# First feed-forward weight loaded and summed one element later; constants of the later stages loaded in the sixth element's round

## The reference, cut to what matters

```python
x = x + _L0_xattn_ref(_layernorm(x, axis=-1), ctx_2048, mask_BxS2_bk0)
x = x + _L0_ffn_ref(_layernorm(x, axis=-1), L0_ffn_w1, L0_ffn_w2, L0_ffn_w3)
x = x + _L1_xattn_ref(_layernorm(x, axis=-1), ctx_2048, mask_BxS2_ik0, L1_xattn_Wq, ...)
x = x + _L1_ffn_ref(_layernorm(x, axis=-1), L1_ffn_wq_gate, L1_ffn_s_gate, ...)
```

```python
def _weight_quant(w):
    scale = 1.0 / jnp.clip(jnp.mean(jnp.abs(w)), EPS)
    return jnp.clip(jnp.round(w * scale), -1, 1) / scale
```

## Time and profile before

| | us |
|---|---|
| Median of 3 runs | 472.57 (471.92 to 473.40) |
| The profiled execution | 470.73 |
| Its span in the trace | 469.0 |
| PE busy | 443.3 (95% of the span) |
| DVE busy | 316.9 (68%) |
| ACT busy | 245.3 (52%) |
| POOL busy | 109.9 (23%) |

### The profile page before, as it was taken

How to read it: one execution, slowest core, us unless ns; L and a number is a source line. 1 busy time by engine, 2 the same in 40 slices (tenths; PEclk the granted TensorE clock), 3 DMA queues, 4 the chain that set the end, 5 groups by cost and what they waited for, 6 DMA issues and landing times.

```text
span 469.0 us, 9959 instructions
## 1 busy us (share of the span) xinstructions
PE 443.3 (95%) x3838; PEld 264.2 (56%) x3847; DVE 316.9 (68%) x574; ACT 245.3 (52%) x370; POOL 109.9 (23%) x126
## 2 busy tenths in 40 slices
PE   8989899999899899999998989799999999999997
PEld 6556565655345355554554777577765565555553
DVE  4995596679857887756765467778876976555211
ACT  4755744764566364555754778576745582222000
POOL 2220400025024000000154377543332252000000
PEclk9999999999999899999999999899999999999999
DMA  8999988934695236633489569977342462000111
GB/s 265 326 381 311 367 282 280 323 105 148 211 289 149 60 82 161 187 87 83 71 300 253 184 212 268 280 262 244 115 140 99 123 179 69 0 0 0 41 59 59
DMA packets 59180, 82.73 MB, mean 176 GB/s; under 512 B 20097, under 2 KB 43649, under 8 KB 57985
## 3 DMA queue, kind: packets, MB, share of 16 engines
q1 hardware_dynamic: 59136, 82.14, 56.8%
q10 hardware_dynamic: 2, 0.01, 0.0%
HBM read 58.76 MB, written 14.42 MB: 156 GB/s over the span
## 4 chain that ended last, share of the span: by engine, by line
PE 68%; DVE 14%; SPq 8%; DMA 4%; issue 3%; ACT 1%; POOL 1%; ACTq 0%; DVEq 0%
PE psum L1598 13%; PE psum L208 8%; PE psum L206 8%; PE psum L1648 7%; PE psum L1431 6%; PE psum L1498 4%; PE psum L673 4%; PE psum L1440 3%; PE psum L1545 3%; PE psum L1528 2%; PE psum L1374 2%; SPq L237 2%; DMA w_stage<-in_w 2%; DMA kst<-k_scratch 2%; PE psum L1392 2%
## 5 line engine op out<-in xcount | busy, mean ns | idle before, releaser
L208 PE MATMUL psum<-wv_p,kv_p 128*128 128x512 f16 x288 | 66.1, 379 | 0.5 <-DVE khl L228 0.5
L206 PE MATMUL psum<-kv_p,wk_p 128*128 128x376 f16 x384 | 66.0, 322 | 0.3 <-DVE khl L228 0.3
L1254 ACT ACTIVATE e<-psum,mask_bias 128x448 f32<-128x448 f32 x96 | 53.4, 640 | 14.9 <-PE psum L1528 13.8
L206 PEld LDWEIGHTS psum<-kv_p,wk_p 128*128 128x128 f16 x384 | 37.5, 98 | 24.6 <-issue 0.6
L208 PEld LDWEIGHTS psum<-wv_p,kv_p 128*128 128x128 f16 x288 | 28.0, 98 | 32.9 <-issue 1.2
L1947 DVE TENSOR_SCALAR e<-e 128x1344 f32<-128x1344 f32 x32 | 33.2, 1038 | 9.4 <-ACT e L1254 9.3
L1598 PE MATMUL psum<-xt,wg_b 128*128 128x448 f16 x176 | 36.9, 352 | 0.3 <-issue 0.3
L1545 PE MATMUL psum<-e,vst 128*32 128x112 f32 x768 | 35.2, 267 | 1.9 <-issue 1.1
L1598 PE MATMUL psum<-xt,wu_b 128*128 128x448 f16 x176 | 36.9, 352 | 0.0
L1294 ACT ACTIVATE gated<-psum,gs 128x448 f32<-128x448 f32 x22 | 13.9, 633 | 39.1 <-PE psum L1598 33.5
L355 POOL TENSOR_SCALAR w_stage<-w_stage,w_stat 128x2816 f32<-128x2816 f32 x6 | 17.1, 2850 | 71.8 <-DVE w_stat L350 71.7
(11 more groups left out here) (198 smaller groups left out, 845.5 us busy)
## 6 DMA issues: line engine op xcount, KB each, us to landing
kst<-k_scratch SPq DMA_DIRECT2D x32, 384.0 KB, 5.9
kv_raw<-in_ctx_feat SPq DMA_DIRECT2D x12, 768.0 KB, 6.1
w_stage<-in_w SPq DMA_DIRECT2D x6, 1408.0 KB, 7.9
cn<-in_ctx_tok SPq DMA_DIRECT2D x8, 768.0 KB, 9.4
k_scratch<-khl SPq DMA_DIRECT2D x128, 48.0 KB, 2.4
v_scratch<-vsp SPq DMA_DIRECT2D x24, 256.0 KB, 2.8
vst<-v_scratch SPq DMA_DIRECT2D x8, 768.0 KB, 7.0
qst<-qhl SPq DMA_DIRECT2D x32, 112.0 KB, 5.4
```

The lines of the kernel that those rows point to most:

```text
L206: mm = pe.matmul(psum[:, kv_bank(p), 0:TQ], wk_p[:, u, k, n * P:(n + 1) * P], src[:, v, k, 0:TQ], **ends)
L208: mm = pe.matmul(psum[:, kv_bank(p), :], src[:, u, k, n * P:(n + 1) * P], wv_p[:, v, k, :], **ends)
L1254: act.activation(e[g][:, c, :], psum[:, D_S + (TC * g + c) % 4, 0:4 * S], ACT.Exp, bias=mask_bias[:, b, c:c + 1], scale=1.0 / (WS * QS)).t ...
```

## The change

In SP's list, w1's first half is loaded in round 0 and its second in round 1, at the place where the second was loaded in round 0 before. w2's halves are loaded at the ends of rounds 3 and 4. The eight constants are issued at the end of round 5. ACT sums w1 in rounds 1 and 2; it sums w2's first half at the end of round 4, now behind the reading of the round's last piece, and the second in round 5 as before. w1 is totalled at the start of round 3, and made ternary in rounds 3 and 4. w2's total stays at the start of round 6.

```diff
@@ SP
-            weight_load(sp, 0, 0, w1)
-            sp.dma_start(attend[:], mask_tok).then_inc(consts_loaded, 16)
...
+            def load_constants():
+                sp.dma_start(attend[:], mask_tok).then_inc(consts_loaded, 16)
...
+                for n, v in enumerate((bo, gamma, beta)):
+                    sp.dma_start(rows3[:, n, :], v.to_broadcast([P, D])).then_inc(consts_loaded, 16)
...
-                if b == 0:
-                    weight_load(sp, 0, 1, w1)
+                if b in (0, 1):
+                    weight_load(sp, 0, b, w1)
...
-                if b in (2, 3):
-                    weight_load(sp, 1, b - 2, w2)
+                if b in (3, 4):
+                    weight_load(sp, 1, b - 3, w2)
+                if b == 5:
+                    load_constants()
@@ ACT
-                if b in (0, 1):
-                    sum_weight(act, 0, b)
-                if b in (4, 5):
-                    sum_weight(act, 1, b - 4)
+                if b in (1, 2):
+                    sum_weight(act, 0, b - 1)
+                if b == 5:
+                    sum_weight(act, 1, 1)
                 for p in A_KV[b][2]:
                     kv_read_hi(act, p)
+                if b == 4:
+                    sum_weight(act, 1, 0)
@@ PE
-                if b == 2:
+                if b == 3:
                     total_weight(pe, 0, A_W)
@@ DVE
-                if b == 2:
+                if b == 3:
                     mean_weight(dve, 0, A_W)
...
-                if b in (2, 3):
-                    ternary_weight(dve, 0, b - 2)
+                if b in (3, 4):
+                    ternary_weight(dve, 0, b - 3)
```

More of the change, by code:

```diff
@@ L792, in _ @@
             load_tok(2)
-            weight_load(sp, 0, 0, w1)
-            sp.dma_start(attend[:], mask_tok).then_inc(consts_loaded, 16)
[L795 to L800, removed]
+            def load_constants():
+                sp.dma_start(attend[:], mask_tok).then_inc(consts_loaded, 16)
+                sp.dma_start(sgu[:, 0, :, 0], sg).then_inc(consts_loaded, 16)
+                sp.dma_start(sgu[:, 1, :, 0], su).then_inc(consts_loaded, 16)
+                sp.dma_start(sdn[:], sd).then_inc(consts_loaded, 16)
+                sp.dma_start(rs_in[:], res_scale.to_broadcast([P, 1])).then_inc(consts_loaded, 16)
+                for n, v in enumerate((bo, gamma, beta)):
+                    sp.dma_start(rows3[:, n, :], v.to_broadcast([P, D])).then_inc(consts_loaded, 16)
             def turn_input(t):
```

## The result

| | before | changed |
|---|---|---|
| Median of 12 runs each, us | 468.89 (466.24 to 473.40) | 470.30 (467.63 to 474.04) |
| Profiled execution, us | 470.73 | 472.68 |
| Its span, us | 469.0 | 471.0 |
| PE busy | 443.3 | 440.6 |

The ratio of changed to before is 1.0074, 95% interval 1.0043 to 1.0106: slower by 3.5 us, between 2.0 and 5.0. That is 1.7 us beyond the top of the forecast's own range for the likeliest case (+1.0, up to +1.8), on the side that I had given 0.38. The ratio counts only executions in the fast state; over all of them the two medians are 1.41 us apart. The forecast of 473.6 was worked out from a median of 472.57 over three executions; over twelve that of before is 468.89, so only differences are compared here.

The account below looks back on a forecast made before the run. PE's own work plus one pause bounds it to about 108 us, then DVE, then PE again. -1.44 + 2.4 = +1.0 on 470.73 gives 471.7; the median lies 1.84 above, so 473.6, range 470.9 to 476.2.

Parts of the forecast that it names:

- the likeliest case: Whole kernel: PE waits 2.4 us at round 6 for w2's late half; +1.0 us, 473.6, range 472.7 to 474.4, chance 0.52.
- the side that I had given 0.38: Whole kernel: slower by over 0.3%, above 473.99 us; chance about 0.38.
- The pause that goes: PE before L341 in round 2: the wait for ACT's sum of w1 does not return in round 3; -1.44 us.
- w2's loads, the step that decides: L341 at round 6: w2's second half lands at 98.6, PE waits 2.4 us; price +2.4.
- the slower rival: L341 at round 6: w2's second half lands much later, at 101; +3.4, so 475.9 us; chance 0.24.
- POOL and DVE in round 3: Round 3: POOL's w1 passes collide with DVE's L248 and L1666; PE waits 0 to 0.7 us, taken as 0.
- The likeliest of the three outcomes: Whole kernel: a time within about 0.3% (1.4 us) of before, between 471.15 and 473.99 us; chance 0.50.
- SP's opening list: Opening: taking the constants (13.6 us of SP) and w1's first half out changes nothing; 0, at most 0.92 us gained.
- The constants in round 5: SP in round 5: eight issues take 3.4 us, up to 13.6, hidden; priced 0, far end +1.
- That rival: SP in round 5: constants issue as slowly as in the opening, delaying w3's sum; +1 on top, 474.6 us; chance 0.06.
- The rival in which the half lands in time: L341 at round 6: w2's second half lands without a wait; 471.1, down to 470.2 us; chance 0.18.

Follow-up runs that it names:

- The filler: The changed kernel with 26 idle products (128x256, results unused) on PE ahead of w2's total at round 6; ratio 1.0018 to the kernel before.
- weights only: The changed kernel with the eight constants loaded in the opening again; ratio 1.0072 to the kernel before, 3.4 us slower.
- w1's half in the opening: The changed kernel with w1's first half loaded in the opening again, its second still in round 1; ratio 1.0051 to the kernel before.
- quarter load: The changed kernel with the DMA of w2's second half cut to 352 of 1408 KB (w2 wrong); ratio 0.9969 to the kernel before.

## Why the prediction was right, and where it was short

- **The pause that goes:** 1.44 forecast, 1.48 measured. L341 of round 3 did not wait.
- **w2's loads, the step that decides:** right in kind. Less the 3.76 of the opening, the first half was issued at 79.3 (79.8 forecast), the second at 88.5 (88.4), ACT started on it at 99.3 (98.6), and L341 ran at 102.0 (101.3). The wait between starts was 3.15 in place of 2.4; sum to here +1.7 in place of +1.0. The 0.7 is the landing: 10.8 us after the issue in place of 10.2. I had added "0 to 1.0" for the late first half and taken 0.3; the run with short POOL passes shows what that lateness was worth: 1.3. By my own reckoning the slower rival decides from a landing of about 99.0 on, and the half landed at 99.3: the case lies on the border of the two.
- **POOL and DVE in round 3:** as played through. L248 2.45, L1672 2.32, POOL 6.70 for its two passes (5.21 before).
- **What was missing:** the clock. I priced PE's pause at its length. In two of three traces of the changed kernel, and in both others that keep the 3 us pause, PE then ran at 0.50 for some 3.5 to 7 us, 0.8 to 1.3 more at the first feed-forward product. I had carried +1.0 to the end because each engine's list is the same from there; behind a new pause the same list does not always take the same time. This, and the 0.7 above, put the timed +3.5 beyond the forecast's own range. With them the sum is +1.7 and 0.8 to 1.3, together 2.5 to 3.0; what is left up to 3.5 is within the interval. The filler's 2.6 us are more than the 0.8 to 1.3 of the traces; two ratios with such intervals don't decide between them.
- **How far the range was luck:** the sign and the place were foreseen, the size was not. The full range of 470.9 to 476.2 reached +3.6 because it took in the slower rival up to its centre, so the measured +3.5 lies inside it by 0.1. The likeliest of the three outcomes was to me no change that can be told (0.50).
- **SP's opening list costed at nothing:** true inside this change, false by itself. I asked which of PE's waits ahead of 30 us hang on a DMA and found none. I should have followed the one wait that I was removing upstream: L341 for ACT, ACT for a DMA issued at 37.62, and SP late with it for the constants and the spills behind them. ACT's wait and the 13.6 us of constants were both in my text, not joined.
- **The constants in round 5:** 5.4 us in place of 3.4, and at 105.4 less the opening in place of 102; hidden, as costed. That rival falls.
- The rival in which the half lands in time did not come; the variants with the half ahead of the features or with a quarter of it come near it. The slower rival had the right place, sign and nearly the size (+3.4), but by a landing at 101 alone, where it was 99.3 and a slower clock.

The version that clearly beats both kernels is the one with the constants alone: 0.9959 to before and, by the two ratios, 0.9886 to the changed one.

## What to carry to other kernels

Before moving a late transfer's consumer, ask why its DMA was issued late: a list of small loads ahead of it in the issuing engine may be the whole cause, and here moving that list cost nothing. A staging buffer that is used in turn hands every delay of one weight on to the next; a round won for the first is a round lost for the second. And a new pause on PE of some 3 us is to be priced with the clock behind it, which a single trace may not show.

## What the runs showed of the hardware

- After a pause of 2.7 to 3.4 us at round 6 PE's granted clock fell to 0.50 in four traces of five (changed kernel twice, weights only, w1's half in the opening) and stayed at 1.00 in the fifth (the changed kernel's first). At that place it stayed at 1.00 in the seven others: without a pause, with one of 0.65 or 1.66 us, or with idle products in it. After a pause of 2.25 us ahead of the first product with w3 it fell in four traces of twelve.
- With the clock at 0.50 for all or most of it, the value piece of round 6 took 4.44 to 5.33 us in place of 2.75; a fall lasted about 3.5 or about 7 us.
- The same first load of 768 KB, with the same loads around it, landed after 4.5 to 6.6 us from one execution to the next, and the openings differed by up to 4 us (by nearly 8 with that of the quarter load, which has a fall of the clock in it).
- A load of 1408 KB issued behind one of 768 KB landed after 10.6 to 11.2 us in the six traces with the loads in that order, whole, and POOL's passes at full length, and after 8.5 with the two exchanged.
- In each of the nine traces with the constants in round 5 seven of the eight issues held SP for 0.43 us and one for 1.2 to 2.0: the first in six of them, a later one in three. In the opening of before the first held it for 0.43 and the others for 0.6 to 2.8 each, 13.6 in all.
